# A one-core transformer block: the prologue's split tiles, ring loads, Hadamard step and first maxima in another order

## The reference, cut to what matters

```python
x = x + attention(layernorm(x), Wq, bq, Wk, bk, Wv, bv, Wo, bo)   # 16 heads of 16
x = x + ffn(layernorm(x), W1, W2, W3)
x = x + gated_memory(layernorm(x), Wv, Wg, bg, Wq, bq, Wo)        # decaying scan over tokens
x = x + ffn(layernorm(x), W1, W2, W3)

def ffn(x, W1, W2, W3):                  # hidden size H = 1024
    hidden = silu(x @ W1.T) * (x @ W3.T)
    hidden = fwht(hidden)                # Walsh-Hadamard transform of 1024, over sqrt(1024)
    return hidden @ W2.T
```

## Time and profile before

| what | value |
|---|---|
| three runs | 675.83, 684.89, 684.90 us (median 684.89) |
| profiled execution, its own time | 675.82 us |
| its span in the trace | 673.8 us |
| its mean granted clock of TensorE | 0.929 |
| TensorE matmul busy | 584.2 us, 87% of the span |
| VectorE, ScalarE, GpSimd busy | 389.6, 302.7, 157.0 us |
| the prologue, to the first product of step K = 0 | 60.63 us |

### The profile page before, as it was taken

How to read it: one execution, slowest core, us unless ns; L and a number is a source line. 1 busy time by engine, 2 the same in 40 slices (tenths; PEclk the granted TensorE clock), 3 DMA queues, 4 the chain that set the end, 5 groups by cost and what they waited for, 6 DMA issues and landing times.

```text
span 673.8 us, 8796 instructions
## 1 busy us (share of the span) xinstructions
PE 584.2 (87%) x3240; PEld 397.7 (59%) x3240; DVE 389.6 (58%) x740; ACT 302.7 (45%) x543; POOL 157.0 (23%) x174
## 2 busy tenths in 40 slices
PE   3645869987798969879699999999999899999997
PEld 2412323432343334324188888888877688888886
DVE  5486566965587737886054544454788743535333
ACT  2313645766467726744733332424443424233331
POOL 1554132342143221570211010101143201010100
PEclk9955986999799968977999999999999999999999
DMA  6993295009300950300010000000000000000000
GB/s 201 126 141 126 35 109 110 2 15 127 49 2 2 116 74 2 126 1 2 14 52 1 1 1 0 1 1 1 1 0 1 0 1 32 1 32 0 32 1 31
DMA packets 17777, 26.51 MB, mean 39 GB/s; under 512 B 2440, under 2 KB 10632, under 8 KB 17352
## 3 DMA queue, kind: packets, MB, share of 16 engines
q1 hardware_dynamic: 16760, 25.18, 20.7%
q10 hardware_dynamic: 976, 0.79, 0.4%
HBM read 10.88 MB, written 5.24 MB: 24 GB/s over the span
## 4 chain that ended last, share of the span: by engine, by line
PE 72%; DVE 8%; ACT 6%; DMA 5%; SPq 4%; issue 4%; POOL 1%; DVEq 0%; ACTq 0%; POOLq 0%
PE PS L249 69%; SPq L185 4%; DVE mxr L743 3%; DMA ring<-mT 3%; ACT PR L622 3%; PE PS L260 3%; DVE XNs L723 1%; DMA ring<-ql 1%; DMA X<-in_x 1%; DVE PR L920 1%; ACT xTh L543 1%; ACT PR L669 1%; ACT xf L543 1%; POOL xTl L951 1%; DVE OT L795 0%
## 5 line engine op out<-in xcount | busy, mean ns | idle before, releaser
L743 DVE TENSOR_REDUCE mxr<-PS 128x1 f32<-128x512 f32 x256 | 164.3, 683 | 85.4 <-PE PS L249 84.0
L249 PE MATMUL PS<-xTh,ring 128*128 128x512 f32 x608 | 193.0, 393 | 2.7 <-POOL xTl L951 2.7
L622 ACT ACTIVATE PR<-PS 128x512 f32<-128x512 f32 x256 | 138.7, 595 | 107.2 <-PE PS L249 106.8
L249 PE MATMUL PS<-ring 48*128 48x512 f32 (+1 forms) x512 | 117.0, 517 | 58.5 <-DMA ring<-mT 18.4
L249 PEld LDWEIGHTS PS<-ring 48*128 48x128 f32 (+1 forms) x512 | 50.2, 208 | 153.8 <-ACT PR L622 53.7
L249 PEld LDWEIGHTS PS<-xTh,ring 128*128 128x128 f32 x608 | 114.2, 189 | 26.9 <-POOL xTl L951 2.9
L249 PE MATMUL PS<-xTl,ring 128*128 128x512 f32 x304 | 114.2, 392 | 0.0
L875 DVE TENSOR_TENSOR PR<-PR,PS 128x512 f32<-128x512 f32 x64 | 43.8, 684 | 92.6 <-PE PS L249 89.8
L543 ACT ACTIVATE AOh<-PR 128x512 fp32r<-128x512 f32 x72 | 45.5, 632 | 108.1 <-DVE PR L875 96.1
L951 POOL TENSOR_TENSOR xTl<-xf,xTh 128x512 fp32r<-128x512 f32 x30 | 43.2, 1453 | 161.5 <-ACT xTh L543 161.5
L249 PE MATMUL PS<-PR,Vp 128*32 128x512 f32 x512 | 78.2, 687 | 2.7 <-ACT PR L622 1.2
(11 more groups left out here) (93 smaller groups left out, 578.7 us busy)
## 6 DMA issues: line engine op xcount, KB each, us to landing
ring<-qh SPq DMA_DIRECT2D x64, 128.0 KB, 5.0
ring<-ql SPq DMA_DIRECT2D x32, 128.0 KB, 5.7
ring<-weight_scratch SPq DMA_DIRECT2D x3, 1024.0 KB, 4.9
X<-in_x SPq DMA_DIRECT2D x4, 512.0 KB, 8.7
weight_scratch<-in_w SPq DMA_DIRECT2D x2, 1024.0 KB, 6.9
out<-X SPq DMA_DIRECT2D x4, 512.0 KB, 2.9
PR<-in_w SPq DMA_DIRECT2D x1, 1024.0 KB, 8.4
ring<-mT SPq DMA_DIRECT2D x32, 8.0 KB
```

Of the source, the lines that this page charges most:

```text
L249: return nc.tensor.matmul(dst, lhsT, rhs, start=start, stop=stop, skip_group_check=True)
L622: nc.scalar.activation(PR[:, j % 8, :], PS[:, KQ0 + j % 3, :], ACT.Exp, scale=HD ** -0.5)\
L743: nc.vector.tensor_reduce(mxr[:, S % 2, blk, TT * p + t:TT * p + t + 1], PS[:, QK0 + i % 3, :], AX.X, ALU.max, negate=True).then_inc(max_d ...
```

## The change

It concerns the prologue alone; the loops behind it keep their order.

- **Four split tiles.** In batch 0 the hi and lo tiles of n = 2 and 3 are slots of `AOh` and `AOl` (`split_tile`), so that ScalarE and VectorE no longer wait for `ring_in`.
- **Two queues.** The four loads of the hi tile of n = 1 are issued by ScalarE, between its tiles n = 1 and n = 2. SyncE issues the others. The three bias loads stand ahead of the ring loads.
- **Butterflies ahead of the product.** The stages run on the raw W2 as soon as it and `had` are loaded, on GpSimd, from `PR[:, 0:4]` to `PR[:, 4:8]`. The four products with `had` read `PR[:, 4:8]` and stand behind U = 8 of the 13 pairs, in the PSUM banks 0, 1, 2 and 6. ScalarE rounds each to `W2h` straight from PSUM, and VectorE subtracts (`scalar_tensor_tensor`) to `W2l` straight from PSUM, behind all 13 `row_max`.
- **First maxima turned early.** The transpose of the first maxima stands behind U = 8, ahead of the products with `had`.
- The statistics of batch 1 stand behind n = 3, its normalisation behind all 13 `row_max`. v is projected into banks 6 and 7. TensorE waits for all of `W2h` and `W2l` before K = 0, instead of ahead of the feed-forward layer.

```diff
@@ -98,6 +98,7 @@
         KQ0, QK0 = 0, 3
+        HAD_BANK = (0, 1, 2, 6)
         OB, MB = PS[:, 6, :], PS[:, 7, :]
@@ -149,6 +150,17 @@
+        def split_tile(b, n, part):
+            t, more = ((qh, AOh), (ql, AOl))[part]
+            return more[:, n % 2, :] if b == 0 and n > 1 else t[:, n % 2, :]
+        def ring_rows(b, n, part):
+            mt, qk = n // 2, n % 2
+            return [(ring[r:r + HD, b % 2, qk, 4 * mt:4 * mt + 4, :].bitcast(F32),
+                     split_tile(b, n, part)[HALF * blk:HALF * blk + HALF, :].bitcast(F32))
+                    for blk in range(2) for r in rows(qk, part, blk)]
         block = ctx.enter_context(nc.Block())
@@ -175,16 +187,12 @@
-            def ring_load(b, n):
-                mt, qk = n // 2, n % 2
-                for part, t, ready in ((0, qh, qk_hi), (1, ql, qk_lo)):
-                    sp.wait_ge(ready, 4 * b + n + 1)
-                    for blk in range(2):
-                        for r in rows(qk, part, blk):
-                            sp.dma_start(ring[r:r + HD, b % 2, qk, 4 * mt:4 * mt + 4, :].bitcast(F32),
-                                         t[HALF * blk:HALF * blk + HALF, n % 2, :].bitcast(F32))\
-                                .then_inc(ring_in[n], DMA)
+            def ring_load(b, n, which=(0, 1)):
+                for part in which:
+                    sp.wait_ge((qk_hi, qk_lo)[part], 4 * b + n + 1)
+                    for args in ring_rows(b, n, part):
+                        sp.dma_start(*args).then_inc(ring_in[n], DMA)
@@ -203,11 +211,11 @@
-            ring_load(0, 0)
-            ring_load(0, 1)
             sp.dma_start(bvt[:, :], bv.partition_broadcast(P)).then_inc(const_in, DMA)
...
             sp.dma_start(bgq[:, :], bgq_d).then_inc(const_in, DMA)
+            ring_load(0, 0)
+            ring_load(0, 1, (1,))
             ring_load(0, 2)
@@ -349,25 +357,26 @@
             for n in range(4):
-                if n == 2:
-                    pe.wait_ge(w2_in, 2 * DMA)
-                    pe.wait_ge(x_f, 2)
-                    for j in range(FT // 2):
-                        last = mm(PS[:, (0, 1, 6, 7)[j], :], had[:, :], PR[:, j, :], True, True)
-                    last.then_inc(had_ready, 1)
                 project_qk(0, n, range(6), PS[:, 2 + n, :])
-            pe.wait_ge(had_copied, 1)
             for half in range(2):
                 for part in range(2):
-                    project_v(0, half, part, PS[:, half, :])
+                    project_v(0, half, part, PS[:, 6 + half, :])
             pe.wait_ge(qk_f, 4)
...
                 score_qk(U)
-            pe.wait_ge(ml_done, 1)
-            nc.tensor.transpose(MB[0:32, 0:P], ms[:, :, :, :].rearrange("p a b k -> p (a b k)"), ident[:, :])\
-                .then_inc(mps_ready, 1)
-            pe.wait_ge(v_copied, 2)
+                if U == 8:
+                    pe.wait_ge(v_copied, 2)
+                    pe.wait_ge(ml_done, 1)
+                    nc.tensor.transpose(MB[0:32, 0:P], ms[:, :, :, :].rearrange("p a b k -> p (a b k)"), ident[:, :])\
+                        .then_inc(mps_ready, 1)
+                    pe.wait_ge(fly_done, 3)
+                    pe.wait_ge(x_f, 2)
+                    for j in range(FT // 2):
+                        mm(PS[:, HAD_BANK[j], :], had[:, :], PR[:, 4 + j, :], True, True).then_inc(had_ready, 1)
+            pe.wait_ge(w2h_done, FT // 2)
+            pe.wait_ge(w2l_done, FT // 2)
@@ -527,7 +536,6 @@
             pe.wait_ge(llo_done, 8)
-            pe.wait_ge(w2l_done, 1)
             pe.wait_ge(max_done, 2 * STEPS * BATCH)
@@ -593,22 +601,22 @@
             for n in range(4):
-                if n == 2:
-                    act.wait_ge(had_ready, 1)
-                    for j in range(FT // 2):
-                        last = hi(PR[:, j, :], PS[:, (0, 1, 6, 7)[j], :], 1.0 / HID ** 0.5)
-                    last.then_inc(had_copied, 1)
                 act.wait_ge(qk_ready, n + 1)
-                if n > 1:
-                    act.wait_ge(ring_in[n - 2], QDMAS)
-                nc.scalar.activation(qh[:, n % 2, :], PS[:, 2 + n, :], ACT.Identity, bias=bqk[:, n:n + 1]).then_inc(qk_hi, 1)
+                nc.scalar.activation(split_tile(0, n, 0), PS[:, 2 + n, :], ACT.Identity, bias=bqk[:, n:n + 1])\
+                    .then_inc(qk_hi, 1)
+                if n == 1:
+                    act.wait_ge(qk_hi, 2)
+                    for args in ring_rows(0, 1, 0):
+                        act.dma_start(*args).then_inc(ring_in[1], DMA)
             for half in range(2):
-                v_evacuate(0, half, PS[:, half, :])
+                v_evacuate(0, half, PS[:, 6 + half, :])
             act.wait_ge(wo_in, 8 * DMA)
             hi(WOh[:, :, :].rearrange("p g n -> p (g n)"), OT[:, :, :].rearrange("p a c -> p (a c)")).then_inc(whi_done, 1)
-            act.wait_ge(fly_done, 3)
-            hi(W2h[:, :, :].rearrange("p f n -> p (f n)"), PR[:, 4:8, :].rearrange("p a n -> p (a n)")).then_inc(w2h_done, 1)
             max_evacuate(0)
+            for j in range(FT // 2):
+                act.wait_ge(had_ready, j + 1)
+                hi(W2h[:, 2 * j:2 * j + 2, :].rearrange("p f n -> p (f n)"), PS[:, HAD_BANK[j], :], 1.0 / HID ** 0.5)\
+                    .then_inc(w2h_done, 1)
@@ -617,8 +625,6 @@
                         act.wait_ge(av_done, K // 2 - 1)
-                    if K == 2 and blk == 0:
-                        act.wait_ge(w2l_done, 1)
                     nc.scalar.activation(PR[:, j % 8, :], PS[:, KQ0 + j % 3, :], ACT.Exp, scale=HD ** -0.5)\
@@ -767,9 +773,6 @@
             for n in range(4):
-                if n == 2:
-                    dve.wait_ge(x_in[1], DMA)
-                    statistics(TT, TT, TT, 2)
                 if n == 0:
@@ -777,14 +780,19 @@
                 dve.wait_ge(qk_f, n + 1)
-                if n > 1:
-                    dve.wait_ge(ring_in[n - 2], QDMAS)
-                lo(ql[:, n % 2, :], qf[:, n % 2, :], qh[:, n % 2, :]).then_inc(qk_lo, 1)
+                lo(split_tile(0, n, 1), qf[:, n % 2, :], split_tile(0, n, 0)).then_inc(qk_lo, 1)
+            dve.wait_ge(x_in[1], DMA)
+            statistics(TT, TT, TT, 2)
             for U in range(LEAD):
                 row_max(U)
-                if U == 8:
-                    dve.wait_ge(rstd_done, 2)
-                    normalise(TT, TT, 1)
+            dve.wait_ge(rstd_done, 2)
+            normalise(TT, TT, 1)
+            for j in range(FT // 2):
+                dve.wait_ge(w2h_done, j + 1)
+                nc.vector.scalar_tensor_tensor(W2l[:, 2 * j:2 * j + 2, :].rearrange("p f n -> p (f n)"),
+                                               PS[:, HAD_BANK[j], :], 1.0 / HID ** 0.5,
+                                               W2h[:, 2 * j:2 * j + 2, :].rearrange("p f n -> p (f n)").bitcast(F32),
+                                               ALU.mult, ALU.subtract).then_inc(w2l_done, 1)
@@ -1002,7 +1010,8 @@
             reciprocal_deviation(0, TT, 1)
-            pool.wait_ge(had_copied, 1)
+            pool.wait_ge(w2_in, 2 * DMA)
             for st in range(3):
@@ -1012,17 +1021,14 @@
             reciprocal_deviation(TT, TT, 2)
-            split_max(0)
             pool.wait_ge(const_in, 3 * DMA)
...
                 place_values(0, g)
+            split_max(0)
             pool.wait_ge(whi_done, 4)
...
                WOh[:, :, :].rearrange("p g n -> p (g n)")).then_inc(wol_done, 1)
-            pool.wait_ge(w2h_done, 1)
-            lo(W2l[:, :, :].rearrange("p f n -> p (f n)"), PR[:, 4:8, :].rearrange("p a n -> p (a n)"),
-               W2h[:, :, :].rearrange("p f n -> p (f n)")).then_inc(w2l_done, 1)
             pool.wait_ge(zero_done, 1)
```

More of the change, by code:

```diff
@@ L118, in build @@
             sem(n) for n in ("one_done", "zero_done", "vone_done", "pool_init", "whi_done", "wlo_done", "wol_done"))
-        had_ready, had_copied, fly_done, w2h_done, w2l_done = (
-            sem(n) for n in ("had_ready", "had_copied", "fly_done", "w2h_done", "w2l_done"))
+        had_ready, fly_done, w2h_done, w2l_done = (
+            sem(n) for n in ("had_ready", "fly_done", "w2h_done", "w2l_done"))
         bst_done, mom_done, veps_done, rstd_done, xns_ready, lnT_ready, x_f, x_hi, x_lo = (
```

## The result

Nine runs each: the kernel before has a median of 679.12 us (674.25 to 684.90), the changed kernel 683.81 us (681.78 to 692.18). The medians are 4.7 us apart. The ratio is 1.0105, with a 95% interval of 1.0061 to 1.0149: slower by about 1%, some 7 us. The ratios in this document are made from fast runs alone, those within 1.5% of the fastest run of the same kernel, which drops the three highest of before here and one of the changed kernel, so a ratio is not the quotient of two medians. The nine runs of before show that its time is not two levels but a spread of 10 us, and that the median of the first three lay at its upper end.

The account below looks back on a forecast made before the run. The prediction took the prologue to be limited by ring-load rate and row-maximum waits, with TensorE nearly full later. + 2.2, + 2.5 and 0.1 rounding gave + 4.8 us: span 678.6, 680.6 with 2.0 around it, forecast 681, range 671 to 693.

Parts of the forecast that it names:

- The sum: Whole prologue: first score pair + 2.2, section behind it + 2.5, 0.1 rounding; loop begins at 65.4, + 4.8 us.
- S: Start of TensorE's first score pair: 34.07 before, predicted 36.3, between 32.4 and 38.7.
- S to the loop: First score pair to main loop: 29.1 us instead of 26.56, so 2.5 us longer.
- Split tiles and two queues: Ring loads before the score pairs: no wait for tile reuse saves 1.69 us; second queue counted as nothing.
- Butterflies first: GpSimd's early butterflies hold VectorE's xTl subtractions, stalling TensorE within n = 0; everything behind moves 3.8 us.
- No stall: Rival: butterflies let VectorE through; first score pair at 32.4, loop at 61.5, 676.7 us; chance 0.17.
- double wait: Rival: VectorE gets in only between pairs of butterflies; first score pair at 38.7, 683 us; chance 0.10.
- Hadamard block: Four products behind U = 8: eight low-clock passes, 3.4 us; pair U = 9 comes 3.2 us later.
- The tail: Last maxima to loop: normalisation and four W2l subtractions make it 4.1 us in place of 2.1.
- From there the order is the same: Behind the loop's start: unchanged order, so the prologue's + 4.8 us carries to the span, 678.6.
- Fast rings: Rival: two queues exceed 124 GB/s, first score pair about 32.5; 677 us, or 670 if the clock holds; chance 0.12.

Follow-up runs that it names:

- e3: Kernel before plus four split tiles, all ring loads from SyncE; ratio to before 0.997 (0.993 to 1.001).
- e4: Kernel before plus four split tiles, ScalarE issuing the four hi loads of n = 1; ratio to before 1.001 (0.996 to 1.005).
- e2: Changed kernel with Hadamard products, W2h, W2l and normalisation ahead of the 13 score pairs; ratio to before 0.997 (0.992 to 1.001).
- e5: Changed kernel with VectorE normalising ahead of the 13 maxima and computing W2l behind U = 8; median 683.62 us, ratio to before 1.001.
- e7: Kernel before with split tiles, earlier statistics, normalisation and maxima handling, one load queue, plus 20 extra TensorE products before the score pairs; ratio to before 0.991.
- e1: Changed kernel with GpSimd's butterflies waiting for all four of VectorE's lo tiles; median 685.87 us, ratio to before 1.000 (0.995 to 1.005).
- e10: Changed kernel with GpSimd's butterflies waiting only for VectorE's two xTl tiles; ratio to before 1.005 (1.000 to 1.010).

## Why the prediction was right and wrong

**The sign and the mechanism were right, the number was set on the wrong level.** The sum said slower by 4.8 us, 0.7% like against like; measured are 1.05%. But the 681 that I gave was the sum on the profiled execution's 675.82, beside a median of 684.89, and read against that median it says faster. The step that failed is the one from the sum to the number: taking 675.83, 684.89 and 684.90 for two levels 9.1 us apart and placing the forecast on the lower one. The nine runs of before show a spread from 674.25 to 684.90 instead, with a median of 679.12. On that median + 4.8 is 683.9, and 683.81 was measured; that it fits so closely is luck, since the sum itself was short. The loop began at 66.91 and 67.36, 6.3 and 6.7 us later than before, where the sum had 65.4 and + 4.8: 0.7 to 1.05 us are missing up to S and 0.8 to 0.9 from S to the loop.

**Split tiles and two queues: right.** The sum had - 1.7 us, e3 and e4 show - 1.4; the second queue brings nothing for S, as taken.

**Butterflies first: right in kind, small by 0.7 to 1.05 us at S.** Predicted: `xTl` ends 19.2, shift 3.8, first ring load 21.2, S 36.3. Measured, second profile and first: 19.2 and 19.6, 21.29 and 21.67, S 37.01 and 37.35. In the first profile the butterflies began at 11.62 (11.17 in the second, 11.1 predicted). In both the twelve loads took 15.6 us instead of 15.0, which no run explains. "No stall" and "double wait" fall with these dates. Each subtraction got the next boundary, as taken.

**Hadamard block: mis-sized.** "At the low clock a pass is 0.43 us, so 3.4 us." I counted the eight records of the earlier trace rows as eight passes at 0.43, which gives nearly the 3.6 us of that row by chance. They ran at the full clock there, as the rows of before around them show:

```profile
18.10 0.80 PE L249 MATMUL PS<-xTl,WAh 128*128 128x512 f32 x2
18.74 3.60 PE L249 MATMUL PS<-PR,had 128*128 128x512 f32 x8
21.77 1.03 PE L249 MATMUL PS<-xTh,WAl 128*128 128x512 f32 x2
22.64 0.62 PE L249 MATMUL PS<-xTh,WAh 128*128 128x512 f32 x2
```

From 18.10 to 18.74 two projections take 0.64 us, one at 0.43 and one at 0.21, so the clock rose there and not at about 22 us. From 18.74 to 22.64 lie 3.90 us: four Hadamard products at 0.86 and two projections at 0.23. In e2 the block takes 3.67 us at a granted 1.00. At the low clock ScalarE's copies show the price of one product, 1.71 us:

```profile
53.79 0.60 ACT L551 ACTIVATE W2h<-PS 128x512 fp32r<-128x512 f32 x1 [1.56 <-PE PS L257]
55.50 0.60 ACT L551 ACTIVATE W2h<-PS 128x512 fp32r<-128x512 f32 x1 [1.11 <-PE PS L257]
56.97 0.60 ACT L551 ACTIVATE W2h<-PS 128x512 fp32r<-128x512 f32 x1 [0.88 <-PE PS L257]
57.83 0.60 ACT L551 ACTIVATE W2h<-PS 128x512 fp32r<-128x512 f32 x1 [0.26 <-PE PS L257]
```

53.79 to 55.50 is 1.71, four times 0.43, and 56.97 to 57.83 is 0.86: the granted clock, 0.50 until 56, rose in between (0.86 in 56:58, 1.00 in 58:60). So a product costs as much as four passes of 512 columns, not two, and the eight passes of the kernel's description are sixteen. The block took 6.07 us, 2.7 more than predicted; wholly at the low clock it would be 6.8 (an estimate, 4 x 1.71). Part of it came back in a way that I had not seen: the granted clock rose while the block ran, and the pairs behind it came 1.34 to 1.36 us apart instead of 1.64.

**The tail: right.** From the last maxima's end (63.56) to the loop 3.8 us; predicted 4.1 (the four subtractions took 2.40 us, the sum had 2.7). e5 confirms its place. S to the loop is 30.0 us instead of 29.1: the pair behind the block came 2.4 later, which the three intervals behind it (0.9), the last maxima and the tail (0.3 each) partly made up.

**"From there the order is the same": right, but not "and so is the time".** T to F differed between two profiles of the same kernel by 6.3 us, beside granted clocks that differed too (last section); what sets them is open.

**Fast rings: refuted** by e3 and e4 for the loads, and by e7 for the clock. The Trainium skill's rule that loads from several engines only save issuing time (DMA: Bandwidth & Descriptors, Issuing engines are not separate DMA queues) holds in these traces: S is 32.69 with one queue and 32.73 with two.

## What to carry to other kernels

Moving work "earlier, where the engine is idle" has a price where its work holds up another engine's, as GpSimd's butterflies did to VectorE's subtractions of two SBUF tiles (5.40 us instead of 1.28 for two): look at what the neighbour does in that window and whether its first result stands at the head of a chain, since a wait of one operation there moves everything, and the same wait behind a backlog costs nothing. Before a block is placed behind a wait of TensorE, price it at the clock of that place, from a row whose clock the rows around it show. A forecast of where a stage begins is best checked at that stage's first row, since a later mark can hold waits of its own. And where runs spread by 1.5%, forecast the difference, and state it against a median of many runs, not against the profiled execution.

## What the runs showed that I had not expected

- One execution differs from another by up to 7.4 us between T and F with the same instructions; the first profile of the changed kernel has a granted mean of 0.70 in 300:340 and 0.66 in 340:360, the second 0.79 and 0.91. The first profile's rows, columns as in the earlier trace rows:

```profile
300.00:340.00 40.00, 33.81 (x154) 12.55 (x154) 19.35 (x35) 20.33 (x40) 12.30 (x14) 0.70 0.01 2
340.00:360.00 20.00, 17.71 (x76) 9.62 (x77) 4.10 (x7) 9.29 (x16) 1.92 (x2) 0.66 0.15 53
```

- The clock's first rise also varies: projections come down from 0.43 to 0.23 us a pass near 16.7 in e1 and near 19.0 in e10, after the same products at the same dates up to there.
- VectorE's held subtraction got in at the next boundary between two GpSimd operations each time, even within a butterfly stage where no semaphore stands, and ended 0.54 to 0.55 us behind it; GpSimd's next operation paid 0.3 to 0.5 us (2.67 to 2.84 instead of 2.35).
